# The first memory read of each half is held back to the twenty-seventh column of VectorE's substitution

## The reference

```python
def step(S, inp):
    q_t, k_t, v_t, b_g, b_beta = inp
    S = S * jnp.exp(b_g)[..., None, None]
    kv = jnp.einsum('mbhk,mbhkv->mbhv', k_t, S)
    dv = (v_t[None] - kv) * b_beta[..., None]
    S = S + k_t[..., :, None] * dv[..., None, :]
    o_t = jnp.einsum('mbhk,mbhkv->mbhv', q_t, S)
    return (S, o_t)
...
_, ys = jax.lax.scan(step, S0, (qt, kt, vt, gt, bt))
```

## Time and profile before

| what | value |
|---|---|
| median of 3 runs | 6611.17 us (6609.73 to 6613.82) |
| the profiled execution | 6641.88 us, span 6640.2 us |
| mean granted TensorE clock | 0.836 |
| DVE busy | 4866.2 us (73%) |
| PE busy | 4427.9 us (67%) |
| POOL busy | 3481.7 us (52%) |
| ACT busy | 3430.4 us (52%) |

### The profile page before, as it was taken

The page is one execution under the profiler, slowest core; times in us unless marked ns, Lnnn a source line. Parts: engine busy times, 40 slices in busy tenths (PEclk is TensorE's granted clock), DMA queues, the critical chain, the costliest instruction groups (busy, mean ns, idle before and its releaser), DMA issues. The chain is left out here.

```text
span 6640.2 us, 196141 instructions
## 1 busy us (share of the span) xinstructions
PE 4427.9 (67%) x78513; PEld 3814.6 (57%) x78513; DVE 4866.2 (73%) x9508; ACT 3430.4 (52%) x6010; POOL 3481.7 (52%) x2081
## 2 busy tenths in 40 slices
PE   1577666667666667666666766666766666655993
PEld 1566566566556666656555665665665665653662
DVE  3788888888888888888888888888888888860003
ACT  1555555565555555555556555555555555631220
POOL 3665555565555665555566555556655556632004
PEclk8788888888888888888888888888888888877996
DMA  2000000000000000000000000000000000012213
GB/s 93 2 6 6 6 6 6 6 6 3 5 6 6 6 6 6 6 6 6 6 6 6 3 5 5 6 6 6 6 6 6 6 6 5 4 46 102 73 59 108
DMA packets 77479, 109.71 MB, mean 17 GB/s; under 512 B 20576, under 2 KB 66208, under 8 KB 75424
## 3 DMA queue, kind: packets, MB, share of 16 engines
q1 hardware_dynamic: 67616, 71.42, 3.3%
q0 software_dynamic: 8960, 25.39, 1.3%
HBM read 57.89 MB, written 38.89 MB: 15 GB/s over the span
## 5 line engine op out<-in xcount | busy, mean ns | idle before, releaser
L1567 POOL TENSOR_TENSOR state<-state,gc_end 128x512 f32<-128x512 f32 x512 | 595.5, 1180 | 1635.1 <-PE bank L595 1577.9
L572 PE MATMUL bank<-state,ke 128*64 128x64 f32 x16384 | 650.2, 247 | 347.1 <-DVE outT L1288 188.2
L572 PEld LDWEIGHTS bank<-state,ke 128*64 128x64 f32 x16384 | 613.6, 160 | 420.5 <-issue 209.2
L608 PE MATMUL last_two<-dvs,kte 128*64 128x64 f32 x16384 | 681.5, 245 | 182.3 <-DVE dvs L1277 180.4
L589 PE MATMUL bank<-rhs,te 128*64 128x64 f32 x8192 | 410.3, 253 | 517.4 <-DVE rhs L1270 284.5
L847 ACT ACTIVATE ke<-kq 32x512 f32<-32x512 f32 x1024 | 643.0, 628 | 198.8 <-DVE kq L1202 185.1
L1251 DVE TENSOR_TENSOR last_two<-last_two,prod 128x31 f32<-128x31 f32 (+15 forms) x1984 | 692.5, 349 | 70.1
L608 PEld LDWEIGHTS last_two<-dvs,kte 128*64 128x64 f32 x16384 | 618.6, 158 | 199.5 <-DVE dvs L1277 187.7
L1249 DVE TENSOR_TENSOR prod<-bd,last_two 128x31 f32<-128x31 f32 (+15 forms) x1984 | 671.2, 338 | 68.3
L797 ACT ACTIVATE te<-tt 32x256 f32<-32x256 f32 x1024 | 422.0, 412 | 568.4 <-DVE tt L1254 557.8
L589 PEld LDWEIGHTS bank<-rhs,te 128*64 128x64 f32 x8192 | 343.4, 162 | 594.9 <-DVE rhs L1270 546.4
(11 more groups left out here) (256 smaller groups left out, 10538.6 us busy)
## 6 DMA issues: line engine op xcount, KB each, us to landing
w_sb<-in_L_ffn_W_dram SPq DMA_DIRECT2D x16, 1024.0 KB, 9.4
expert_rows<-ke SPq DMA_DIRECT2D x1, 8192.0 KB, 21.9
xrows<-expert_rows SPq DMA_DIRECT2D x16, 512.0 KB, 8.4
expert_outputs<-yrow POOLq DMA_DIRECT2D x16, 512.0 KB, 3.3
xt<-_attn_hidden_states_dram SPq DMA_DIRECT2D x32, 128.0 KB, 2.8
xr<-_attn_hidden_states_dram SPq DMA_DIRECT2D x32, 128.0 KB, 2.1
x_after_attention<-xr SPq DMA_DIRECT2D x32, 128.0 KB
xo<-x_after_attention SPq DMA_DIRECT2D x32, 128.0 KB
```

Of the source, the lines that this page charges most:

```text
L572: mm = pe.matmul(bank_mem[g][s, q % 4 * DK:q % 4 * DK + DK], ke[:, c, r, q, s], state[:, hh * HQ + q, r, :], start=(r == 0), stop=(r == 1))
L608: mm = pe.matmul(bank_upd[g][s, (q % 4) * P + r * DK:(q % 4) * P + r * DK + DK], kte[:, r, q, s], dvs[:, q, :], start=True, stop=True)
L1567: pool.tensor_tensor(sv, sv, gc_end[:, vh, 4 * g:4 * g + 4, c].unsqueeze(2).broadcast_to([P, 4, 2 * DK]), ALU.mult).then_inc(sem(f"state_f ...
```

## The change

A new semaphore `solve_ends` is raised by VectorE in each of the 64 solves, ahead of column 26 (that is when the second instruction of column 25 has ended), with an instruction of its own. TensorE waits for it ahead of the first memory read of each of the 63 halves that have one. Since the signal of solve number v (counted from 0) brings it to v + 1, the wait of half u = v + 1 is for the solve that VectorE ends half v with.

```diff
@@ -663,6 +663,7 @@
                 if hh == 1:
                     pe.wait_ge(sem("logits_taken"), since("logits_taken", n))
                 if not first:
+                    pe.wait_ge(sem("solve_ends"), v + 1)
                     memory_read(v, vh, 0)
                     corrections(v, vh, 0)
                     update_and_outputs(v, 0)
@@ -1243,6 +1244,8 @@
                 for j in range(C - 1):
                     for do in meanwhile.get(j, ()):
                         do()
+                    if j == 26:
+                        dve.sem_inc(sem("solve_ends"), 1)
                     rows, cols = C - 1 - j, j + 1
                     pr = prod[:, 0:rows * cols].rearrange("p (i c) -> p i c", c=cols)
                     below = t_prob[:, j + 1:C, 0:cols]
```

## The result

The changed kernel takes 6643.23 us (median of 6, 6640.22 to 6645.15); beside it on the same chip the kernel before takes 6612.49 us (6606.22 to 6619.38). The ratio is 1.0046 with a 95% interval of [1.0034, 1.0059], so the change costs about 31 us. I had forecast 6610 us and no difference that can be measured. It is slower, outside my range.

What follows compares the result with a forecast made beforehand. VectorE, the busiest engine, was taken as the bound, with its solve a serial chain. Signal 7.4, warmer corrections -9.2, Gram-matrix loss +1 sum to -0.8 us: 6610 us from the median, range 6596 to 6624 us (gain-only range 6602 to 6617).

Steps and rivals of the forecast that it cites:

- The signal: In VectorE's 64 solves, one exposed instruction each of 0.115 us: 7.4 us cost, with bounds zero and 7.4 us.
- another alignment: Rival: shifted halves change L1138 and L1143 beside GpSimd, up to some 20 us either way; chance 0.08 faster, 0.07 slower.
- The step on the gain: Short halves' corrections start at TensorE's high clock: 0.42 us saved in each of 22 halves, 9.2 us; bounds nothing to 27.
- the read is hidden in both kinds of half: Chunk 0's later memory read ends before VectorE wants it, over 2 us early in short halves, 4 us behind the turn.
- the gap between read and corrections: In short halves TensorE's idle time ahead of the corrections drops from 7.36 us to about 2.9 us.
- nothing lost or won behind the turn: In the 30 loop-turn halves corrections begin 4.9 us after the read and stay slow: nothing gained, nothing lost.
- All short halves warm: Rival: the whole 0.83 us wait at the corrections goes in all 33 short halves, giving 6591 us; chance 0.08.
- Only the signal counts: Rival: the corrections' gain fails or is lost at the Gram matrices, leaving the signal's 7.4 us: 6618.6 us; chance 0.22.
- The read comes too late: Rival: the read ends over 2.2 us later than reckoned, so VectorE's right sides wait; 0.6 us gives 6638 us; chance 0.05.

Runs made afterwards that it cites:

- run with one instruction ahead of the loop: Kernel before plus one bare VectorE signal ahead of the loop, nothing added inside it and nobody waiting for it: 1.0020 [1.0011, 1.0029], 13 us more.
- wait three columns later: TensorE's wait on `v_chain` set to the end of column 28 instead of column 25, no added signals: 1.0012 [1.0003, 1.0021] against the kernel before.
- two alone: Kernel before plus 2 bare VectorE signals at its idle start, ahead of the wait for the weights: 0.9997 [0.9988, 1.0006].
- wait-only kernel: Kernel before plus TensorE's wait on `v_chain` for the end of column 25's second instruction, no added signals: 0.9984 [0.9975, 0.9993], 10.6 us less.
- shifted change: Whole change plus 127 bare VectorE signals at its idle start, ahead of the wait for the weights: 0.9988 [0.9979, 0.9997] against the kernel before.
- shifted kernel with signals only: Change with all 64 signals and 127 more at VectorE's start, without TensorE's wait: 1.0002 [0.9993, 1.0011] against the kernel before, 1.3 us more.
- signal only: Kernel before plus the signal ahead of column 26 in all 64 solves, without TensorE's wait: 1.0041 [1.0027, 1.0055], 27 us more.

## Why the prediction was wrong

**The step that failed** is "*The signal*": "64 x 0.115 = 7.4 us", and with it "Its bounds are zero and this." The price of one signal was right (0.115 us in the solve). But I costed the signal as a duration only, and the bound as if the durations of other instructions did not depend on how many stand ahead of them. The signals measured 27 us in place of 7.4. Their parts:

- Own length: 7.1 us in the solves of the profile after. With the stream put back, the kernel with signals measured 1.3 us over the kernel before (-5 to +7); L1139 and L1144 together took 2.3 us less there, which hides a part.
- Pauses: at L1289 in the half behind the turn 0.25 us more than the usual 0.03, at L1254 in the solve 0.15 more; 0.40 x 31 iterations = 12.3 us. The run with one instruction ahead of the loop has them without any signal in the loop, and measured 13 us (7 to 19); its profile has the pair below 4.3 us longer as well, so this isn't the price of the pauses alone.
- The pause ahead of L1149 costs nothing itself and takes the cover from the corrections: VectorE comes 0.36 us later and waits that much less.
- L1139 and L1144, beside GpSimd: 65.6 us together before (26.1 and 39.5), 70.0 after (46.1 and 23.9). This is the part of my rival "another alignment" that happened, 4.4 us of its 20; the pair took 68.0 to 71.2 us in the six kernels with pauses at L1289 and in the solve, and 58.5 to 65.6 in those without, except the wait three columns later (69.4).
- 5 to 9 us of the 27 stay open. The two kernels with signals only, unshifted and shifted, differ by 0.39% or 26 us, and in their profiles by 22.4 us up to the last half; the pauses explain 12.3 of it and the pair 5 (68.5 and 63.3). Most of the rest lies between chunk 3's right sides and the Gram matrix's transposition, 4.6 us longer than before in the unshifted kernel and 1.2 us in the shifted one; why was not followed up. The signals displace the earlier part of an iteration by one place and the later part by two; one alone gave 13 us and two alone nothing. What both do together wasn't tried, and the intervals (6 us on either side) leave room for a part of it.

**The step on the gain was right in size, and failed on where it holds.** I had 9.2 us for the corrections, and the stretch over them shrank by 9.0 us in the wait-only kernel. That the whole time came out close too, 10.6 us less (1 to 0.9984) and 9 us less in the shifted change (1.0002 to 0.9988), is in part luck: the pair L1139 and L1144, for which I had no direction, took 5.7 us less in the first, and 4.8 us less in the second than in the shifted kernel with signals only. In the stream as the change leaves it, it gave nothing that can be measured: signal only 1.0041, change 1.0046; with one instruction, 1.0020 and 1.0023. The profiles show two things that take it. The pause ahead of L1149 leaves only 0.48 of the 0.83 us to win; and the corrections start at 0.50 in 25 of 33 short halves of the changed kernel (29 when run again), in place of 8 in the wait-only kernel. Why fewer halves are warm stays open. The length of the gap alone isn't it: in the wait-only kernel it is 2.78 us on average and 25 windows stand above 0.50; with the one instruction ahead of the loop it is 2.76 us, and there are 10.

**Right**: the read is hidden in both kinds of half, no right side waits for it anew; the gap between read and corrections; nothing lost or won behind the turn by the wait itself (12.023 and 12.016 us from the first to the second right sides). A small term had been left out: the read now runs beside the solve's transposition, which takes 1.920 us in place of 1.894, 1.6 us in all.

**The rivals.** "All short halves warm" did not happen: 25 windows at best rose, none of them wholly, and with the read three columns later 13 halves were wholly warm and the kernel was slower. "Only the signal counts" named the right instruction, at 7.4 us; that is about its price where the places are put back (1.3 us by the runs, -5 to +7, and 5.7 us in the profile up to the last half), and not in the change. The Trainium skill ("TensorE: Matmul & The Clock Gate", Part 1) advises short gaps. With 2.7 us the kernel here was faster (0.9984); with 1.27 us it was not (1.0012), although the corrections were warm in 13 halves. "The read comes too late" did not happen. The Trainium skill's sentence that a semaphore costs nothing extra ("VectorE: DVE Perf Modes", The DRAIN you can't avoid) holds for the wait on `v_chain`, which is raised by instructions that run anyway (0.9984); the bare signal, an instruction of its own, is another matter (0.115 us each in the solve).

The two best kernels are the wait on `v_chain` alone, 0.9984, and the change shifted by 127, 0.9988. The first needs no padding and is the one to keep.

## What to carry to other kernels

When an edit adds instructions to the engine that bounds the kernel, cost not only their length but what they displace: here each 128th place of VectorE's program is a pause, free beside a long instruction or ahead of a wait, and 0.15 to 0.25 us each time in the two places where nothing hid it. Cost also where the displaced instructions fall against GpSimd's: the same two lines took 58 to 71 us in all. Before adding a signal, look for a counter that existing instructions raise already, and before judging an edit by its time, run it once more with padding at an idle place, which separates the edit from its displacement. A gain from a warmer TensorE has to be followed through the next chunks, since the clock can be low at a dearer place afterwards.

## What the runs showed of the hardware

**Pauses at every 128th instruction of VectorE.** 127 dummy instructions at the start moved a kernel from 1.0046 to 0.9988, 128 left it at 1.0048; the pauses found in the traces are 128 places apart. In the changed kernel the instruction at such a place starts 0.42 to 0.48 us behind the record ahead of it, each time; in the shifted kernel the same five take 0.21, 0.29, 0.09, 0.07 and 0.40 us. So the pause costs what is missing to about 0.44 us. That it is the supply of instructions which stops there is my inference, from the period and from the missing releaser; no run measured the supply itself.

**VectorE instructions that last as long as GpSimd's.** L1139 takes 0.28 us by itself and up to 1.98 us beside a GpSimd instruction of 1.90 us, and ends 0.07 us behind it.

**Unexplained stops in the last half.** In the profiles of the kernel before and of the first eight experiments the last half's right sides span 60.6 to 62.6 us, in those of the change and of the last three experiments 39.6 to 40.5 us, and the medians of the kernel before moved along: 6638 and 6639 us beside the eight, 6613 and 6612 us beside the others. In the long ones TensorE stops every few matmuls with nothing to wait for; the cause is not known. A profiled execution can thus stand 30 us off the median, as the one that I started from did; I had noted that distance and not asked where it lay.
